# Zero products on TensorE in its waits, and the residual rows added later, in a two-layer decoder

## The reference

```
x = x + attn(layernorm(x))             # layer 0: causal, rotary, 16 wide heads
x = x + xattn(layernorm(x), ctx, ctx)  # 77 context rows
x = x + moe(layernorm(x))              # one of 8 experts by argmax, 256 -> 1024 -> 256, relu
x = x + attn(layernorm(x))             # layer 1: 64 wide heads, not causal
x = x + xattn(layernorm(x), ctx, ctx)
x = x + ffn(layernorm(x))              # itself two parts:
    h = x + attention(rmsnorm(x))      # 16 wide heads, not causal
    h = h + moe(rmsnorm(h))            # top 2 of 8 experts, 256 -> 512 -> 256, silu gate
```

## Time and profile before

| | us |
|---|---|
| median of three runs | 2990.66 |
| profiled execution | 2986.54 |
| its span, first to last instruction | 2984.9 |
| TensorE busy | 2419.0 (81%) |
| VectorE busy | 1588.0 (53%) |
| ScalarE busy | 1155.4 (39%) |
| GpSimd busy | 984.6 (33%) |
| mean granted TensorE clock | 0.886 of full |

### The profile page before, as it was taken

How to read it: one execution, slowest core, us unless ns; L and a number is a source line. 1 busy time by engine, 2 the same in 40 slices (tenths; PEclk the granted TensorE clock), 3 DMA queues, 4 the chain that set the end, 5 groups by cost and what they waited for, 6 DMA issues and landing times. The chain is left out here.

```text
span 2984.9 us, 46600 instructions
## 1 busy us (share of the span) xinstructions
PE 2419.0 (81%) x15980; PEld 1321.5 (44%) x15980; DVE 1588.0 (53%) x2548; ACT 1155.4 (39%) x2075; POOL 984.6 (33%) x836
## 2 busy tenths in 40 slices
PE   3748996575899697799999998858739999847996
PEld 3613434234788475233333332733512222246885
DVE  2758873437233332666666663233658999553223
ACT  1516664242000232344444444224416777711221
POOL 0831003301222111576777776130560000003331
PEclk7959998576999898899999999866869999968998
DMA  3442212432564576122222221543451121024555
GB/s 110 100 89 59 59 38 67 80 72 90 168 211 159 180 195 188 51 77 83 86 77 84 82 78 42 155 73 71 109 102 55 31 57 34 8 76 154 197 195 175
DMA packets 250865, 299.71 MB, mean 100 GB/s; under 512 B 64174, under 2 KB 196948, under 8 KB 250196
## 3 DMA queue, kind: packets, MB, share of 16 engines
q1 hardware_dynamic: 221684, 227.59, 26.2%
q0 software_dynamic: 27104, 68.49, 8.6%
q10 hardware_dynamic: 1920, 1.57, 0.3%
HBM read 205.49 MB, written 91.25 MB: 99 GB/s over the span
## 5 line engine op out<-in xcount | busy, mean ns | idle before, releaser
L1749 ACT ACTIVATE a_probs<-a_cols 128x512 f32<-128x512 f32 (+3 forms) x896 | 445.2, 549 | 239.1 <-PE a_cols L1680 162.1
L1770 DVE TENSOR_REDUCE a_mxw<-a_rows 128x2 f32<-128x1024 f32 (+1 forms) x448 | 475.4, 1099 | 70.6 <-PE a_rows L1638 42.3
L2196 DVE TENSOR_REDUCE a_mxw<-a_rows 128x2 f32<-128x1024 f32 x256 | 313.3, 1224 | 208.3 <-PE a_rows L2034 206.6
L2174 ACT ACTIVATE a_probs<-a_cols 128x1024 f32<-128x1024 f32 x256 | 261.9, 1025 | 266.7 <-PE a_cols L2063 249.6
L2015 POOL TENSOR_TENSOR a_sums<-a_sums,a_probs 128x1024 f32<-128x1024 f32 x128 | 309.6, 2419 | 100.3 <-ACT a_probs L2174 87.1
L1680 PE MATMUL a_cols<-a_qs,a_ks 50*128 50x512 bf16 (+7 forms) x1792 | 275.4, 363 | 17.6 <-DMA a_qs<-a_nparts 11.5
L2450 PE MATMUL e_psU<-e_xT,e_w 128*128 128x256 f32 x1216 | 273.8, 384 | 1.9 <-ACT e_xT L2497 1.2
L2059 PE MATMUL a_cols<-a_qf,a_kf 64*128 64x512 f32 x1024 | 266.5, 598 | 0.0
L522 PE MATMUL t_psP<-t_xT,t_wf 128*128 128x256 f32 x1024 | 236.6, 389 | 36.7 <-ACT t_xT L615 18.1
L1638 PE MATMUL a_rows<-a_ks,a_qs 48*128 48x512 bf16 (+3 forms) x896 | 174.3, 385 | 111.9 <-DMA a_ks<-k_scratch 68.1
L1708 PE MATMUL a_out<-a_probs,a_vs 128*17 128x256 f32 (+4 forms) x3328 | 255.6, 380 | 0.2 <-ACT a_probs L1749 0.2
(11 more groups left out here) (248 smaller groups left out, 3045.7 us busy)
## 6 DMA issues: line engine op xcount, KB each, us to landing
e_w<-in_w SPq DMA_DIRECT2D x69, 512.0 KB
e_w<-in_w SPq DMA_DIRECT2D x30, 1024.0 KB
qk_wide_scratch<-t_f SPq DMA_DIRECT2D x32, 512.0 KB, 2.9
q_scratch<-t_parts POOLq DMA_DIRECT2D x128, 96.0 KB, 2.4
a_qs<-q_scratch SPq DMA_DIRECT2D x96, 128.0 KB
a_qs<-q_scratch SPq DMA_DIRECT2D x168, 64.0 KB, 2.3
a_ks<-k_scratch SPq DMA_DIRECT2D x144, 64.0 KB, 2.6
vw_scratch<-t_v SPq DMA_DIRECT2D x16, 520.0 KB, 7.2
```

Of the source, the lines that this page charges most:

```text
L1749: act.activation(pr[ug % RING][:, 2 * hp + e, c0:512], psC[(2 * at + e) % 3][:, 0:512 - c0], ACT.Exp, scale=scale).then_inc(ex_done, 1)
L1770: dve.tensor_reduce(mxw[w][:, a, :, hp, t % 4:t % 4 + 1], src[:, :, 0:n], AX.X, ALU.max).then_inc(s_free, 1)
L2174: act.activation(pr[i][:], psC[i % 2][:], ACT.Exp, scale=scale).then_inc(ex_done, 1)
L2196: dve.tensor_reduce(mxw[:, j % 2, :, j // 2:j // 2 + 1], psR[:], AX.X, ALU.max).then_inc(s_free, 1)
```

## The change

It is called on TensorE with 512 columns each time:

```
# token_stage
+        warm = st.ps("warm", [P, 512]) if RP == 2 else psP[RP - 1]
 ...
                     if front:
                         c, p, r = front
+                        if gate is not None:
+                            zero_products(pe, G, warm[:], 6)
                         pe.wait_ge(xn_ready, c + 1)
 ...
                         mm.then_inc(turned, 1)
+                        if not attn and isinstance(c, int) and c == 0:
+                            zero_products(pe, G, warm[:], 20)
+                if attn:
+                    zero_products(pe, G, warm[:], 12)
                 in_stages(pe, NC, step)
# narrow_attention_stage
+                zero_products(pe, G, psO[:], 24)
                 if causal:
                     pe.wait_ge(masks_set, 1)
                 for slot in prologue():
                     run(slot)
+                    n = steps[slot[2]][slot[3]][3] if slot[0] == "step" else 0
+                    zero_products(pe, G, psO[:], 3 * n // 512)
 ...
-                pe.wait_ge(out_zeroed, 1)
 ...
-                dve.memset(psO[:], 0.0).then_inc(out_zeroed, 1)
# moe_stage, TensorE
                 mm.then_inc(inverted, 1)
+                zero_products(pe, G, psU[3][:], 20)
# moe_stage, VectorE
                 signal(indices_ready)
-                op(dve.tensor_tensor(X[:], X[:], G["Y"][:], ALU.add))
 ...
                         dve.tensor_copy(yo[p][:], psD[p][:]).then_inc(y_ready, 1)
+                    if isinstance(j, int) and j < 2:
+                        for q in (2 * j, 2 * j + 1):
+                            some = slice(q * QUARTER, (q + 1) * QUARTER)
+                            dve.tensor_tensor(X[:, some, :], X[:, some, :], G["Y"][:, some, :], ALU.add)
```

More of the change, by code:

```diff
@@ L225, in _ @@
                 dve.memset(G["zeros"][:], 0.0)
+                dve.memset(G["zerosb"][:], 0.0)
                 for n, name in enumerate(whole_numbers):
@@ L1501, in narrow_attention_stage @@
         ones_set = [st.sem("first_ones_set"), st.sem("other_ones_set")]
-        out_zeroed = st.sem("out_zeroed")
         s_ready, s_free = st.sem("rows_ready"), st.sem("rows_free")
@@ L2666, in decoder @@
         G["spare"], G["zeros"] = g.sb("spare", [P, 2, n_pieces(2) * R // P]), g.sb("zeros", [P, 2 * NT * E])
+        G["zerosb"] = g.sb("zerosb", [P, 512], BF16)
         G["eps"], G["tick"] = g.sb("eps", [P, 1]), g.sb("tick", [1, 1])
```

## The result

The kernel after takes 2980.12 us (median of 20 runs, 2974.55 to 2995.36) against 2994.47 us before (20 runs, 2983.32 to 3004.54), both measured together. The ratio is 0.9957, 95% interval 0.9945 to 0.9968, so the change takes off 12.9 us, interval 9.6 to 16.5. The forecast was 18.7 us. As a time it was 2972 us, with a range of 2961 to 2985; 2980.12 lies inside it, 8.1 us above the forecast, of which 3.8 us is the kernel before itself: its 20 runs have a median of 2994.47 where the three that the forecast started from had 2990.66. The profiled executions of this measurement span 2980.4 and 2984.9 us. They stand only 4.5 us apart, because that execution of before was one of its fastest and the after's a middling one. I therefore read single places from the profiles and sums from the medians.

The account below looks back on a forecast made before the run. TensorE sets the pace mid-stage at full clock, VectorE in gate stages; stage beginnings run at low clock. Terms 7.5 - 1.0 + 2.3 + 1.0 + 6.8 + 2.3 + 0.3 - 0.5 = 18.7 us off 2986.5; median forecast 2972, range 2961 to 2985.

Parts of the forecast that it names:

- Step 1: Starts of e6 and e2: without the residual addition ahead, the first gather takes 1.0 us; gains 4.0 and 3.5, sum 7.5.
- Step 2: Addition moved in quarters behind pieces 0 and 1 of e2 and e6: 0.2 to 0.3 us per piece, cost 1.0.
- Step 3: Starts of e6 and e2: zero products raise the clock; gain 2.3 us net in e6 and 1.0 in e2.
- Step 6: Narrow attentions: zero products at the start and prologue steps; a5 gains 0.3 us, a0 loses 0.5.
- step 5: Gate stages t2 and t6: six zero products per step gain 0 in the middle, 2.3 us at the ends.
- step 4: Beginnings of the token stages: zero products raise the clock there; gain 6.8 us in sum.
- the rival of a gather's own 5 us: e2 and e6: the 5 us belong to the first gather itself; 7.5 us lost, 2979.5 us; chance 0.13.
- the weights' traffic: e2: the gather lands behind queued weights, which may swallow some of the 4.0 us; 3.5 taken, bounds 0 and 4.0.
- the hold behind the zeros: e6: zero products end after the transpose could start, holding it about 1.0 us, bounds 0 and 2.6.
- the second rival: The clock falls again in every pause between zero products and real work; 2980 us, chance 0.15.
- longer prologue steps: Narrow attentions: a sign that the forecast is wrong; a three-zero step was priced at 1.7 us low clock, 0.86 full.
- The third rival: Gate steps and narrow attentions' prologues: products of zeros do not raise the clock; +31 us, 3022 us, chance 0.07.

Follow-up runs that it names:

- Kernel 3: The kernel after plus a 4.4 us one-input VectorE reduction at the addition's old place; one execution, 2975.58 us.
- kernel 7: kernel 4 with piece 1's weight loads in the expert stages issued once both gathers of piece 0 have landed; 2970.25 us, ratio 0.9924.
- kernel 8: kernel 7 with more zero products at the starts of t0, t3, t4 and t6; 2968.89 us (ratio 0.9917), second run 2965.33 us (0.9915).
- kernel 9: kernel 8 with the narrow attentions' zero products back: all of them 2967.16 us (ratio 0.9920), or only the 24 at their start 2970.23 us (0.9931).
- kernel 4: The kernel after without zero products in a0 and a5, psO cleared by VectorE again; 2973.83 us, ratio 0.9939.
- kernel 5: The kernel after with only the 24 zero products at the start of a0 and a5, none at the prologue steps; 2977.44 us, ratio 0.9950.
- kernel 6: The kernel after without the 6 zero products ahead of each step of gate stages t2 and t6; 2981.42 us, ratio 0.9968.

## Why the forecast was too high

The direction and the mechanisms of steps 1 to 3 were right; the sum was 5.8 us too large. Step 6 and the end of t2 in step 5 had the mechanism wrong, step 4 was too large because the clock fell in pauses. By the steps of the prediction:

**Step 1, gathers, 7.5.** Right in e6: 4.0 forecast, 3.97 measured (5.01 to 1.04). Kernel 3 and the products of line 2621 show the reason, the two SBUF inputs, and the rival of a gather's own 5 us fell. The hold is one of the indirect DMA alone: 18 of GpSimd's direct stores of `parts` in t0 of the kernel after start beside a two-SBUF-input operation that runs 0.35 to 1.14 us longer, and they take 0.62 to 0.65 us like the others. In e2 3.5 was forecast and 3.1 came. The prediction had named the weights' traffic as the risk and sized it too small; kernel 7 shows that it was just this, and that another 4.6 us of e2 could be had by issuing the weights later.

**Step 2, the quarters, -1.0.** Right: 0.20 and 0.19 per piece in e6, 0.26 twice in e2, in all 0.9. That a held scatter costs nothing also held. The first scatter behind a quarter took 1.72 us and not 1.00, the hold of step 1 once more:

```profile
2715.64 1.72 POOL L2416 DMA_INDIRECT results_scratch<-e_y,e_to  x1 [10.36 <-DVE e_y L2629]
```

**Step 3, zeros in the expert stages, 2.3 and 1.0.** e6 was better: to the end of the first piece 7.0 us are gone where steps 1 and 3 had 6.3 (4.0 + 2.3). The clock gain of 0.5 + 2.8 came to the tenth, the hold behind the zeros was 0.3 and not 1.0 (4.50 us from the gather's start, where 8.18 less 3.97 would be 4.2). In e2 nothing came: the zeros ended at 747.2 and 4.3 us of pause followed, the landing of step 1 again. Where the pause was 0.3 or 0.4 us (kernel 8, second run, and kernel 9 with the 24) the clock stayed, and e2 took 250.9 and 251.0 us, against 252.6 us in the two others of experiments 8 and 9, where it fell.

**Steps 4 and 5, token stages, 6.8 and 2.3.** Of 9.1 about 5.6 came: the seven token stages sum to 697.3 us in the mean of six profiles with these zeros (694.2 to 699.9), against 702.8 in two without (701.2 and 704.5). With so much scatter 5.6 is an estimate that can be 2 or 3 us off. Three things are missing.
The pauses are the first: in t0 and t4 the clock rose and fell again before or just behind the first product. This was the second rival; it holds in part. With the pauses filled (four profiles of kernels 8 and 9) the sum is 693.0 (690.2 to 695.5).
The second is t2's end. The prediction took it that nothing covers the last gate. GpSimd's last row store does: it starts with the gate, and e2 begins 4.35 us behind the store's start, in the kernel before and in kernel 4 alike, though the gate took 1.85 us in the one and 1.03 in the other:

```profile
722.95 0.71 POOL L442 DMA_DIRECT2D rows_scratch<-t_z  x1 [5.10 <-DVE t_z L720]
...
727.30 0.06 DVE L2514 MEMSET e_earlier<- 128x1 f32 x1 [2.37 <-PEq L154]
```
```profile
715.91 1.03 PE L539 MATMUL t_psP<-t_wg,t_xT 128*128 128x8 f32 x8 [0.89 <-DVE g_logits L797]
715.98 0.71 POOL L450 DMA_DIRECT2D rows_scratch<-t_z  x1 [5.09 <-DVE t_z L734]
...
720.33 0.06 DVE L2529 MEMSET e_earlier<- 128x1 f32 x1 [3.18 <-PEq L160]
```

The distance is 4.34 or 4.35 us in eleven of the thirteen profiles (5.0 and 5.4 in the others), so the 0.9 us could not have come.
The third is the same store at the end of t6. Its last gate ran in 1.06 us instead of 1.88 and its last transposes in 0.66 instead of 1.12, and most of these 1.28 us did not reach e6, as these rows of the kernel after show:

```profile
2670.45 0.71 POOL L450 DMA_DIRECT2D rows_scratch<-t_xn  x1 [3.83 <-DVE t_xn L721]
...
2671.55 1.06 PE L539 MATMUL t_psP<-t_wg,t_xT 128*128 128x8 f32 x8 [0.69 <-ACT t_xT L629]
```
```profile
2674.81 0.06 DVE L2529 MEMSET e_earlier<- 128x1 f32 x1 [2.00 <-PEq L160]
```

From the gate's end at 2672.61 to e6 it is 2.2 us; in the kernel before it was 1.2 (2671.61 to 2672.8). From the start of GpSimd's last row store to e6 it is 4.4 us, as in t2, and 4.7 before (2668.17). So the store now ends this stage too, and of the 1.28 us 0.98 stays behind the barrier. This is read from the traces; moving the store was not tried.

**Step 6, the narrow attentions, +0.3 and -0.5.** This is the step whose mechanism failed, and the prediction's own sign of it, longer prologue steps, came. By the stages' means it is off by 3.6 us; by the prologues' windows alone, where the two together cost 1.6 to 3.8 us in a profile, by 1.4 to 3.6. I had priced a step with three zeros at 1.7 us at the low clock; it takes 1.93, and the profile has three of these in a5 and five slowed ones in a0. But the size was not the mistake. In a prologue that VectorE sets, a higher clock can give nothing, so the zeros there could only cost; the gain that I set against it, the first value products behind the prologue, did not come either, as the clock fell at 187.9 and 2239.3, just ahead of the first products of the main loops at 190.3 and 2241.1; so it did in all five kernels with these zeros. Kernels 4 and 5 come out faster at the medians without the steps' zeros, kernel 9 does not (0.9931 with the 24 alone, 0.9920 with all); no difference among these is clear of the intervals.

The third rival, zeros that do not raise the clock, fell at once: 24 zero products behind 25 us of idle time in a0 began at 160.67, and the clock went from 0.50 to 1.00 at 164.0, still within them. The Trainium skill ("TensorE: Matmul & The Clock Gate", section "What's actually happening") names no dependence on data, and the trace agrees with it there.

The accounts then stand so, forecast against what the runs give: gathers and quarters 6.5 and 6.2; zeros in the expert stages 3.3 and 3.0; token and gate stages 9.1 and 5.6; narrow stages -0.2 and -3.8. The second set sums to 11.0, the medians say 12.9 with an interval from 9.6. The last two accounts are means of single executions and uncertain by some us each; they stand 3.5 and 3.6 us under the forecast.

The best kernel by its ratio is the change without its narrow zeros, with piece 1's weights behind the gathers and with the pauses filled: 0.9917 and 0.9915, some 25 us off the kernel before and nearly twice the change. The interval of its first run (0.9900 to 0.9933) lies clear of the change's, but not of kernel 7's nor of kernel 9's.

## What to carry to other kernels

Filler work raises the clock, but it pays only where TensorE sets the pace behind it and where it lasts until the real operands are there: look at the pause between the last filler product and the first real one, and at who sets the pace of the steps. Keep VectorE operations with two SBUF inputs away from the indirect transfers that start a stage. When a step on the path gets shorter, look up at once what it lands in: here the next weights in e2, and a row store in front of e2 and e6.

## What the runs showed of the hardware

- An indirect DMA on GpSimd is held until a VectorE addition of two SBUF inputs ends: 5.00 and 5.01 us in e2 and e6, against 1.03 and 1.04 beside a one-input reduction of the same 4.42 us. It works both for gathers and for scatters (1.72 against 1.00 us). Beside a product with one input in PSUM it is not held (at most 1.00 us in 281 cases), and GpSimd's direct stores are not held beside two SBUF inputs (0.62 to 0.65 us, 18 cases).
- Behind zero products the clock fell to 0.50 around pauses of 3.5 us (t0), 3.8 (t4), 4.3 (e2) and 2.2 (t6) in the kernel after, and of 2.7 (t4) in kernel 8; one of 2.5 us in t3 did not bring it down, nor did 2.7, 2.8 and 3.1 us in t0 of kernels 5, 4 and 6. So the same pause can go either way. In e2 even 0.9 to 1.4 us did, where a second wait of 1.2 us, for ScalarE, follows the transposes at once; 0.3 to 0.4 us did not. Each fall in the kernel after put 3.4 to 6.8 us at the low level.
- In t0 a fall is worth 2 us of the stage: 117.4 to 118.6 us where the clock held, 119.6 to 120.8 where it fell.
- A product of zeros of 128x512 takes 0.43 us at the low and 0.21 at the full clock; three in a row beside 48-row products cost 1.46 and 0.82 us.
- The main loops meet stretches of low clock at places that change from execution to execution: a1, which no kernel of these changes, took 122.3 us with the clock low in 74.5 us of it, and 132.9 with 105.4. A stage of one profile says nothing on a few microseconds.
